# A decoder layer's attention: causal scores in three tiles a step, and the early block's high half copied by VectorE

## The reference

```python
c_q   = hidden @ w_q_down                       # 384 wide
c_kv  = hidden @ w_kv_down                      # 128 wide, shared by all 32 heads
q_lat = einsum('bhsd,hdr->bhsr', q_nope, wuk)   # 128 wide per head
scores = einsum('bhsr,btr->bhst', q_lat, c_kv) + einsum('bhsd,btd->bhst', q_rope, k_rope)
scores = where(causal, scores / sqrt(192), min) # causal: lower triangle of 128 x 128
out_lat = einsum('bhst,btr->bhsr', softmax(scores), c_kv)
out = (out_lat per head @ w_uv) @ w_out
```

## Time and profile before

| | before |
|---|---|
| median of 3 runs | 1919.72 us (1919.02 to 1920.83) |
| span of the profiled execution (first to last instruction) | 1917.3 us |
| TensorE matmul / weight load busy | 1909.2 / 1615.0 us |
| VectorE / ScalarE / GpSimd busy | 1531.8 / 1168.9 / 1048.7 us |
| loads of `qrope` | 128 DMAs of 256 KB, median 5.3 us to landing |
| share of the 16 DMA engines | 58.0% |

### The profile page before, as it was taken

One profiled execution on the slowest core, in us unless ns is written; L12 is line 12 of the kernel. 1 busy time (PEld: TensorE's weight loads), 2 busy tenths in 40 slices (PEclk: granted clock), 3 DMA queues, 4 the chain that ended last, 5 costly groups with the idle time before them and its releaser, 6 DMA issues.

```text
span 1917.3 us, 32648 instructions
## 1 busy us (share of the span) xinstructions
PE 1909.2 (100%) x10048; PEld 1615.0 (84%) x10048; DVE 1531.8 (80%) x2655; ACT 1168.9 (61%) x2648; POOL 1048.7 (55%) x891
## 2 busy tenths in 40 slices
PE   9999999999999999999999999999999999999999
PEld 7888888888888888888888888888888877888887
DVE  6778888888888887877777777777878889996677
ACT  5456767676758575765555555555656668766441
POOL 5468777787869696865555556555565511000000
PEclk9999999999999999999999999999999999999999
DMA  9838474647474655588546264464628286466645
GB/s 361 333 105 317 133 260 130 253 125 263 122 266 138 231 171 199 195 319 328 181 151 233 77 230 132 158 207 140 217 82 302 91 285 250 198 220 245 229 152 176
DMA packets 86473, 393.13 MB, mean 205 GB/s; under 512 B 9472, under 2 KB 10240, under 8 KB 67328
## 3 DMA queue, kind: packets, MB, share of 16 engines
q1 hardware_dynamic: 86400, 392.21, 58.0%
HBM read 236.46 MB, written 155.71 MB: 205 GB/s over the span
## 4 chain that ended last, share of the span: by engine, by line
PE 97%; DVE 2%; DMA 1%; ACT 0%; issue 0%; DVEq 0%; POOL 0%; ACTq 0%; SPq 0%
PE at_out L1281 11%; PE at_out L1285 10%; PE at_out L1282 10%; PE at_qbank L55 7%; PE at_qbank L57 7%; PE at_qbank L56 7%; PE at_score L1244 6%; PE at_score L1235 3%; PE at_turned L1256 3%; PE at_qbank L1605 3%; PE at_score L1605 2%; PE at_out L1605 2%; PE at_value L56 2%; PE at_value L55 2%; PE at_value L57 2%; PE at_qbank L1608 2%
## 5 line engine op out<-in xcount | busy, mean ns | idle before, releaser
L2620 DVE TENSOR_TENSOR at_acc<-at_out,at_acc 128x512 f32<-128x512 f32 x640 | 438.9, 689 | 138.2 <-PE at_out L1285 136.2
L2266 POOL TENSOR_TENSOR at_acc<-at_stage,at_acc 128x512 f32<-128x512 f32 x256 | 332.3, 1298 | 184.1 <-ACT at_stage L1747 174.5
L1281 PE MATMUL at_out<-at_wvo,at_val_hi 128*128 128x512 f32 x896 | 365.3, 408 | 0.5 <-ACT at_stage L1747 0.2
L1285 PE MATMUL at_out<-at_wvo,at_val_lo 128*128 128x512 f32 x896 | 350.6, 391 | 0.0
L1282 PE MATMUL at_out<-at_wvo,at_val_hi 128*128 128x512 f32 x896 | 350.5, 391 | 0.0
L1747 ACT ACTIVATE at_stage<-at_out 128x512 f32<-128x512 f32 x256 | 153.0, 599 | 125.2 <-PE at_out L1285 112.9
L1787 ACT ACTIVATE at_pT_hi<-at_turned 128x512 fp32r<-128x512 f32 x128 | 76.4, 597 | 245.8 <-PE at_turned L1256 245.8
L2226 POOL TENSOR_TENSOR at_probs<-at_probs,at_row_stats 128x512 f32<-128x512 f32 x128 | 133.3, 1041 | 148.2 <-DVE at_row_stats L2582 148.2
L1781 ACT ACTIVATE at_probs<-at_probs,at_row_stats 128x128 f32<-128x128 f32 x512 | 197.7, 388 | 8.8 <-DVE at_row_stats L2577 8.8
L1285 PEld LDWEIGHTS at_out<-at_wvo,at_val_lo 128*128 128x128 f32 x896 | 168.4, 188 | 37.8
L1281 PEld LDWEIGHTS at_out<-at_wvo,at_val_hi 128*128 128x128 f32 x896 | 169.1, 189 | 31.1 <-DVE at_acc L2620 5.7
(11 more groups left out here) (313 smaller groups left out, 4772.3 us busy)
## 6 DMA issues: line engine op xcount, KB each, us to landing
parts_d<-at_rope_tmp SPq DMA_DIRECT2D x32, 1024.0 KB, 6.1
at_qrope<-parts_d SPq DMA_DIRECT2D x128, 256.0 KB, 5.3
wvo_d<-at_wvo SPq DMA_DIRECT2D x16, 2048.0 KB, 7.8
at_wvo<-wvo_d SPq DMA_DIRECT2D x16, 2048.0 KB, 8.1
ff_w_d<-ff_w SPq DMA_DIRECT2D x21, 1024.0 KB, 6.2
ff_w<-ff_w_d SPq DMA_DIRECT2D x21, 1024.0 KB, 4.8
ab_raw<-in_w_heads SPq DMA_DIRECT2D x32, 576.0 KB, 5.5
wvo_d<-at_wvo SPq DMA_DIRECT2D x16, 1024.0 KB, 9.8
```

What stands on the lines that cost most here:

```text
L1281: pe.matmul(out, hi, weight[:, 0], start=start, stop=False, skip_group_check=True)
L1285: pe.matmul(out, lo, weight[:, 0], start=False, stop=True, skip_group_check=True).then_inc(out_ready, 1)
L2266: pool.tensor_tensor(at, stage[group][z][:], at, ALU.add).then_inc(pool_added, 1)
L2620: dve.tensor_tensor(at, outb[FACTORS[name][2]][:], at, ALU.add).then_inc(added, 1)
```

## The change

Causal queries 0 to 63 of a batch see only keys 0 to 63. The change divides each batch's queries into an early half (0 to 63) and a late half (64 to 127). A late tile holds the late halves of both heads of a batch against all 128 keys; there are two, one per batch. The third tile holds the early halves of both heads: batch 0 against its keys 0 to 63 in columns 0 to 63, batch 1 in columns 64 to 127. So there are three tiles of 128 x 128 and three transposes. The queries are laid out by half, head and token (`qlat`, `qrope`), and the loads of `qrope` become sixteen DMAs with runs of 64 floats. After the turn the early block of batch 0 stands in partitions 0 to 63, that of batch 1 in partitions 64 to 127; both go to partitions 0 to 63 of `pT_hi` and `pT_lo`, whose other half is set to zero once. ScalarE copies the late tiles (256 columns) and batch 0's early block (128 columns, 64 partitions). VectorE itself copies batch 1's early block, and then takes the low parts in three instructions. The order of the value's quarters changes with it; their numbers and sizes stay.

```diff
 def relayout_in(m, c):
     for j in range(4):
-        sp.dma_start(as_f32(qrope[c][j * HALF:(j + 1) * HALF]), of[SLOT_OF_PART[j]]).then_inc(qrope_in[c], 16)
+        for h in range(QUAD):
+            to = as_f32(qrope[c][j * HALF:(j + 1) * HALF, h // PAIR, :, h % PAIR])
+            sp.dma_start(to, of[SLOT_OF_PART[j]][:, h].rearrange("p (k q) -> p k q", q=HQ)).then_inc(qrope_in[c], 16)

 def score_ropes(m, s, group):
     for bl in range(2):
-        for h in range(PAIR):
-            pe.matmul(score[:, bl * PAIR + h], qrope[c][:, pair * PAIR + h, cols], rope_keys[:, :, cols],
-                      start=h == 0, stop=False, skip_group_check=True)
+        pe.matmul(score[:, bl], both_heads(qrope[c][:, pair, half_of(s, bl, 1)]), rope_keys[:, :, batch_cols(s, bl)],
+                  start=bl == 0, stop=False, skip_group_check=True)
+    for bl in range(2):
+        pe.matmul(score[:, EARLY, :, early_keys(bl)], both_heads(qrope[c][:, pair, half_of(s, bl, 0)]),
+                  rope_keys[:, :, early_cols(s, bl)], start=bl == 0, stop=False, skip_group_check=True)

 def score_rests(m, s, taken):
-    (four matmuls of 128 columns)
+    for bl in range(2):
+        pe.matmul(score[:, bl, 0], both_heads(qlat[u % 2][:, half_of(s, bl, 1)]), compressed[c][:, batch_cols(s, bl)], ...)
+    for bl in range(2):
+        ins = pe.matmul(score[:, EARLY, 0, early_keys(bl)], both_heads(qlat[u % 2][:, half_of(s, bl, 0)]),
+                        compressed[c][:, early_cols(s, bl)], ...)

 def turn(m, s):                                             # TensorE
-    for j in range(PARTS):
-        to = TURNED_AT[j]
-        ins = pe.transpose(turned[:, to * SEQ:(to + 1) * SEQ], probs[s % 2][:, j, :], ident[:])
+    for to, tile in enumerate((1, 0, EARLY)):
+        ins = pe.transpose(turned[:, to * SEQ:(to + 1) * SEQ], probs[s % 2][:, tile, :], ident[:])

 def exps(m, s):                                             # ScalarE, j of 4
+    rows = probs[i][:, j, :] if j < EARLY else probs[i][:, EARLY, early_keys(j - EARLY)]

 def turn(m, s):                                             # ScalarE
-    act.activation(pT_hi[:], turned[:], ACT.Copy).then_inc(pT_hi_done, 1)
+    act.activation(pT_hi[:, :, HQ:SEQ], late_turned, ACT.Copy).then_inc(pT_by_act, 1)
+    act.activation(pT_hi[0:HQ, heads_at(0), 0:HQ], early_turned[0], ACT.Copy).then_inc(pT_by_act, 1)

 def normalise(m, s):                                        # GpSimd
-    (one product of 512 columns)
+    (one of 2 x 128 columns, one of 2 x 64)

 def largest(m, s, which=range(3)):                          # VectorE
-    (mask on 512 columns, addition on 512, maximum on 512)
+    (mask on 2 x 128 and 2 x 64, addition on 3 x 128, maximum on 2 x 128 and 2 x 64)

 def turn(m, s):                                             # VectorE
-    dve.wait_ge(pT_hi_done, STEPS * m + s + 1)
-    dve.tensor_tensor(pT_lo[:], turned[:], as_f32(pT_hi[:]), ALU.subtract).then_inc(pT_lo_done, 1)
+    done = 2 * (STEPS * m + s)
+    def early(bl):
+        to = slice(0, HQ), heads_at(bl), slice(0, HQ)
+        return dve.tensor_tensor(pT_lo[to], early_turned[bl], as_f32(pT_hi[to]), ALU.subtract)
+    dve.wait_ge(pT_by_act, done + 1)
+    dve.tensor_copy(pT_hi[0:HQ, heads_at(1), 0:HQ], early_turned[1]).then_inc(pT_by_dve, 1)
+    dve.wait_ge(pT_by_dve, 2 * (STEPS * m + s) + 1)
+    early(1)
+    dve.wait_ge(pT_by_act, done + 2)
+    dve.tensor_tensor(pT_lo[:, :, HQ:SEQ], late_turned, as_f32(pT_hi[:, :, HQ:SEQ]), ALU.subtract)
+    early(0).then_inc(pT_by_dve, 1)

 def opening():                                              # VectorE
+    dve.memset(as_f32(pT_both[HQ:P, :, :, 0:HQ]), 0.0)
```

More of the change, by code:

```diff
@@ L136, in decoder, with high @@
     PRODUCTS, PLAIN = 7, 3
[L137 to L142, removed]
+    BLOCKS = PRODUCTS + 1
+    A21, A22, A11, A12, S2, S3, S4, S1 = (slice(j * SEQ, (j + 1) * SEQ) for j in range(BLOCKS))
+    DIRECT, SUMS = slice(SEQ, 4 * SEQ), slice(4 * SEQ, BLOCKS * SEQ)
+    A11_A12, S3_S4 = slice(A11.start, A12.stop), slice(S3.start, S4.stop)
+    HQ, HALVES = SEQ // 2, 2 * BPC
+    LATE, EARLY = slice(0, 2), 2
+    TILES = 3
+    def high(of):
+        return slice(of.start - SEQ, of.stop - SEQ)
     FACTORS = {"P1": (A11, "b11", 0), "P2": (A12, "b21", 1), "P6": (S2, "t2", 0), "P5": (S1, "t1", 0),
@@ L316, in decoder @@
         prep_turned = outb[1]
+        late_turned = turned[:, 0:2 * SEQ].rearrange("p (k q) -> p k q", q=HQ)
+        early_turned = [turned[bl * HQ:(bl + 1) * HQ, 2 * SEQ:3 * SEQ].rearrange("p (k q) -> p k q", q=HQ) for bl in range(2)]
         cr_turned, cr_out = qbank, [turned, value]
@@ L396, in batch_cols, with early_cols, half_of, both_heads @@
             return slice(b * SEQ, (b + 1) * SEQ)
+        def early_cols(s, bl):
+            return slice(batch_cols(s, bl).start, batch_cols(s, bl).start + HQ)
+        def half_of(s, bl, late):
+            return 2 * (2 * (s % 2) + bl) + late
+        def both_heads(of):
+            return of.rearrange("p h q -> p (h q)")
+        def early_keys(bl):
+            return slice(bl * HQ, (bl + 1) * HQ)
+        def heads_at(bl):
+            return slice(PAIR, 2 * PAIR) if bl == 0 else slice(0, PAIR)
         def place(s):
@@ L809, in preparation @@
                 relayout(0, 0)
-                sp.wait_ge(qrope_in[0], 64)
+                sp.wait_ge(qrope_in[0], 256)
                 sp.wait_ge(prep_turn_taken, lo_at["x", KT * N - 1] + 1)
@@ L1241, in score_rests @@
                 for bl in range(2):
[L1242 to L1245, removed]
+                    pe.matmul(score[:, bl, 0], both_heads(qlat[u % 2][:, half_of(s, bl, 1)]), compressed[c][:, batch_cols(s, bl)],
+                              start=False, stop=True, skip_group_check=True)
+                for bl in range(2):
+                    ins = pe.matmul(score[:, EARLY, 0, early_keys(bl)], both_heads(qlat[u % 2][:, half_of(s, bl, 0)]),
+                                    compressed[c][:, early_cols(s, bl)], start=False, stop=True, skip_group_check=True)
                 ins.then_inc(score_ready, 1)
@@ L1278, in product @@
                 val, op, n = FACTORS[name]
-                out, hi, lo, weight = outb[n][:], val_hi[s % 2][:, val], val_lo[s % 2][:, val], wvo[pair][op]
+                out, hi, lo, weight = outb[n][:], val_hi[s % 2][:, high(val)], val_lo[s % 2][:, val], wvo[pair][op]
                 pe.matmul(out, hi, weight[:, 0], start=start, stop=False, skip_group_check=True)
@@ L3090, in constants @@
         "ident": np.eye(P, dtype=np.float32),
-        "mask": np.where(np.tril(np.ones((SEQ, SEQ), bool)), 0, MASKED).astype(np.float32),
+        "mask": np.concatenate([np.zeros((P, SEQ // 2)), np.tile(np.where(np.tril(np.ones((SEQ // 2, SEQ // 2), bool)), 0, MASKED),
+                                                                  (2, 1))], axis=1).astype(np.float32),
         "cos": np.tile(cos * root, (QUAD, 1)),
```

73 lines of the change are left out of this document (40 added, 33 removed).

## The result

The changed kernel takes 1960.67 us (median of 4 runs, 1960.23 to 1962.56) against 1920.28 for the kernel before on the same chip: ratio 1.0211, 95% interval 1.0197 to 1.0225. The profiled execution spans 1958.5 us, 41.2 more than before. 1912.4 was forecast, and the range ended at 1931.

The account below looks back on a forecast made before the run. The kernel was taken as bound by TensorE's queue of matmuls, almost without holes. -16.6 + 1.0 + 7.3 + 1.0 = -7.3 against the profiled span of 1917.3 gave 1910.0, plus 2.4 made 1912.4 us; range 1903 to 1931.

Parts of the forecast that it names:

- On its way VectorE works longer in the turn: VectorE after the transposes: four operations in place of one, +0.3 to +0.5 us per turn.
- I count it at zero: Chain from scores to probabilities: some 0.4 us shorter, its effect counted as zero except in the full quads.
- holes before the values in the later quads: Sign of being wrong: the chain from the turn would be longer than the 0.60 us spare allows.
- TensorE's part: Each step: one transpose fewer and slightly cheaper narrow matmuls save 0.13 us, times 128 steps -16.6 us.
- the floor of 0.11: Narrow rotary and latent matmuls: each takes at least 0.11 us, the time its 128-column weight load occupies TensorE's load path.
- the third rival: Narrow matmuls run by their columns: 1872 us, chance 0.06, of which 0.01 for a skill figure of 81 ns per matmul.
- -1.04 + 0.15 + 1.2 = +0.3: Per full quad: TensorE's saving, +0.15 us net at the transposes and turn, +1.2 us for late raw rotary weights.
- x: ScalarE's wait for late raw rotary weights in six full quads: 0.1 to 3.9 us, taken as 0.8.
- the first rival: Raw rotary weights late by all of 3.9 us at ScalarE in six quads: 25.8 in place of 7.3, 1931 us, chance 0.30.
- the rule on runs under 512 B: Relayout loads with 256 B runs: below line rate, SP's queue would not drain, ScalarE's wait would be 3.9 us.
- Nothing lost, 1.2 us left: Later quads: rotary weights land later behind sixteen SP issues, but 1.2 us stays spare before TensorE wants them.
- 7.3 + 0.7: Sixteen SP issues: +7.3 us over six full quads, including the longer chain's share, and 0.7 once in the switch quad.

Follow-up runs that it names:

- e1: Changed kernel with 64 drains (instructions that compute nothing) at the start of VectorE's program; 1924.94 us, ratio to before 1.0027.
- e2: Changed kernel with the rotary queries' relayout in 4 stores and 4 loads, in place of 1 store and 16 loads; 1971.75 us.
- e5: Changed kernel with the relayout in 4 stores and 4 loads and 64 drains at the start of VectorE's program; 1913.72 us, ratio to before 0.9970.
- e9: Changed kernel with only 8 drains at the start of VectorE's program; 1921.09 us, ratio to before 1.0012.
- e11: Changed kernel with the relayout in 4 stores and 4 loads and 8 drains at the start of VectorE's program; 1911.41 us, ratio to before 0.9953.
- e8: Kernel of e2 with SP holding the second relayout's loads until VectorE is through its first turn behind the return; 1958.00 us.
- e3: Kernel before the change with 7 more semaphore increments per step in VectorE's later loop and 140 drains at its program's start; 1989.93 us, ratio 1.0365.
- e10: Changed kernel with the relayout in 4 stores and 4 loads and ScalarE copying both batches' early blocks, without drains; 1945.39 us, ratio to before 1.0134.
- e7: Changed kernel with 220 drains at the start of VectorE's program and nothing else; 1959.33 us.

## Why the prediction was wrong

**The step that failed** is the counting of VectorE's new instructions. "On its way VectorE works longer in the turn" priced them by their durations alone (+0.3 to +0.5 us a turn), and "I count it at zero" followed. VectorE has room for them in time: 67.0 of 84.2 us busy in a later quad. What they broke is where its loop lies in its code. None of the rivals had it. The prediction had "holes before the values in the later quads" among its signs of being wrong, and they came, but it tied them to a chain from the turn that is too long; e1 has the same chain and no such hole. The six returns account for 33.3 + 6 x 1.04 = 39.5 of the 48.5 us between forecast (-7.3) and result (+41.2). Most of the rest lies in the first later quad and behind the last one. The trace of before could have raised the question, as it has 34 packets on queue 14 and none of them in the last six later quads.

The Trainium skill has the rule, on its page "Runtime: NRT & Kernel Launch" (Instruction fetch mechanics): the code memory of engines other than TensorE holds 512 instructions and is refilled in blocks of 256, and a taken branch to a target outside the two blocks held must fetch it before the engine goes on. The runs agree in every row of the table. They do not settle how large a piece is: pieces of 128, of which a loop may touch three, give the same rows with 62 to 65 instructions ahead. For the price, 3.9 to 11.0 us of idle VectorE at a return here, the page has no number.

**TensorE's part: right.** One score block of a later quad, for the earlier trace rows:

```profile
1115.81 0.40 PE L1260 MATMUL at_score<-at_tok,at_qrope 128*128 128x256 f32 x2
1116.04 0.34 PE L1263 MATMUL at_score<-at_tok,at_qrope 128*128 128x128 f32 x2
1116.21 0.51 PE L1284 MATMUL at_turned<-at_ident,at_probs 128*128 128x128 f32 x3
1116.57 0.61 PE L1270 MATMUL at_score<-at_keys,at_qlat 128*128 128x128 f32 x4
1117.01 0.56 PE L1273 MATMUL at_score<-at_keys,at_qlat 128*128 128x64 f32 x4
1117.38 0.48 PE L1309 MATMUL at_out<-at_wvo,at_val_hi 128*128 128x512 f32 x1
```

The block takes 1117.38 - 1115.81 = 1.57 us, where it took 1.72. Successive narrow latent records end 0.112 us apart and the narrow rotary ones 0.115: the floor of 0.11 holds, and the third rival, matmuls by their columns, is out, with the 81 ns that it names. 0.04 of the 0.15 does not reach the step. A free later quad goes from 83.04 to 82.17 us, so -0.11 per step where -0.13 was said: -14 us and not -16.6.

**The full quads: right in the sum by luck, wrong in the parts.** Forecast per quad: -1.04 + 0.15 + 1.2 = +0.3. Measured: 92.1 to 92.6 against 92.05 to 92.24, +1.5 over six, where 6 x 0.3 = 1.8 were forecast; the errors below cancel. Sixteen issues take 7.9 us (7.6 was said); the raw rotary weights land 3.3 us after issue (median; 7.2 before), the short end, and ScalarE waits for them:

```profile
616.97 0.84 ACT L1907 ACTIVATE at_wqr<-at_rope_tmp 128x768 fp32r<-128x768 f32 x1 [0.16 <-DMA at_rope_tmp<-in_w_rope]
```

Over the six quads x is 0.3 on average (1.6 us in all) and not 0.8, so the first rival is out, and with it the x = 3.9 that the prediction had from the rule on runs under 512 B. Together with the later turn it costs 0.35 to 0.8 us before the values of the fourth step, which e2 and e5 no longer lose. The chain at the third step costs 0.5 (0.15 was taken). The latent queries wait 0.3 and 0.45 us for their bank, where before they did not in these quads.

**"Nothing lost, 1.2 us left" in the later quads: wrong in the first one.** There TensorE does wait for the rotary weights; in the six others it does not, and not only because VectorE's stall hides it: in e1, which has no stall there, the weights are in time in these six.

```profile
893.71 0.49 PE L55 MATMUL at_qbank<-at_tok,at_wqr 128*128 128x512 f32 x1 [1.67 <-DMA at_wqr<-wqr_d]
```

**What was not looked at: the end of the attention.** SP goes from the last relayout to the loads of the next stage, and one of their readers stands in VectorE's queue of the last quad:

```profile
1507.45 0.69 DVE L2836 BATCH_NORM_STATS2 cr_stats<-cr_x 128x6 f32<-128x512 f32 x1 [3.52 <-DMA cr_x<-x_d]
```

TensorE then waits 3.7 us for an addition behind it. With eight issues (e2, e5) the wait is gone. e1 to e5, both free of VectorE's stall, is 1924.9 to 1913.7, and e9 to e11 is 1921.1 to 1911.4: 10 to 11 us are what the sixteen issues cost the whole kernel, where 7.3 + 0.7 had been forecast, for fewer places and with a part of the longer chain in it.

## What to carry to other kernels

Instructions added to a loop have a price beside their durations: count the loop's instructions on each engine, see where they lie, and look whether the trace has instruction packets in the steady state. When an engine idles on "issue" right behind its loop's return, shift its code by a few instructions before touching the work; eight drains were worth 40 us here. And follow a queue that gets longer past the end of its loop, to the first loads of the next stage.

## What the hardware showed that was not expected

- Code travels with the data: a return left VectorE idle for 3.9 to 4.2 us with idle queues (e8), 4.9 to 5.3 beside sixteen paced loads (changed kernel) and 7.4 to 8.5 beside denser ones (e2); in e3, 9.5 to 11.0. Making the loads' issue cheaper made the kernel slower until the code was shifted.
- The second hole stands where the table puts a border. The later loop of the changed kernel starts 4 instructions ahead of one (956 + 64 = 1020, and the border is 1024), and its second hole comes behind its first 4 instructions, two of them operations. The full loop of e10 starts 7 ahead (505, the border is 512), and its second hole comes behind 7, five of them operations:

```profile
433.25 0.42 DVE L2631 TENSOR_TENSOR at_pT<-at_turned,at_pT 128x256 fp32r<-128x256 f32 x1 [4.70 <-issue]
...
437.28 0.56 DVE L2612 TENSOR_TENSOR at_probs<-at_score,at_probs 128x384 f32<-128x384 f32 x1 [2.46 <-issue]
```

  In e3 the 8 instructions ahead of the border compute nothing, and there is one long hole. In e7 the full loop starts 34 ahead and has one hole of 4.1 to 5.1 us. That fits a second fetch which is in time if there are enough instructions to run before the border; no run varied this distance alone.
- Why the first later quad of e1 is 86.9 us and that of e9 84.7 is open: the rotary weights come 3.3 and 2.2 us late, and in e1 output weights 1.3 us behind them, though both kernels load alike.
